# Batch 0 of an adaLN block: modulation of the first batch computed on all partitions, and a new order of its work

## What is computed

```python
mod = (_silu(L0_c) @ L0_wmod).reshape(L0_c.shape[0], 6, 1, -1)
sa, ca, ga, sb, cb, gb = (mod[:, 0], ..., mod[:, 5])
ga = (2 * (ga >= 0) - 1) * jnp.maximum(jnp.abs(ga), 0.25)      # gb likewise
h = _layernorm(x, axis=-1) * (1 + ca) + sa
x = x + ga * attn(h)     # attn: layernorm(gamma, beta), Q K V = h @ W_in + b, rotary on K and V,
                         # A = sum over rows of cos_sim(K) * cos_sim(V), (0.5 * A + 0.5) * Q @ W_out + b, + h
h = _layernorm(x, axis=-1) * (1 + cb) + sb
x = x + gb * ffn(h)      # relu(h W_up) W_down + sum(top-2 softmax weights) * (h W_expert)
```

## Time and profile before

| | us |
|---|---|
| median of 3 runs | 402.54 |
| the runs | 398.53, 402.54, 403.09 |
| the profiled execution | 401.57 |
| its span, first to last instruction | 399.8 |
| PE busy in it | 357.4 |
| DVE, ACT, POOL busy | 250.6, 169.4, 114.2 |
| mean granted clock of TensorE | 0.96 |

### The profile page before, as it was taken

How to read it: one execution, slowest core, us unless ns; L and a number is a source line. 1 busy time by engine, 2 the same in 40 slices (tenths; PEclk the granted TensorE clock), 3 DMA queues, 4 the chain that set the end, 5 groups by cost and what they waited for, 6 DMA issues and landing times.

```text
span 399.8 us, 4571 instructions
## 1 busy us (share of the span) xinstructions
PE 357.4 (89%) x1620; PEld 280.7 (70%) x1620; DVE 250.6 (63%) x512; ACT 169.4 (42%) x307; POOL 114.2 (29%) x114
## 2 busy tenths in 40 slices
PE   4639773099999799998999999999999999999996
PEld 0138462088788588886878887888788878887886
DVE  0784490766998848888597846863852556074454
ACT  1364740858441772117611775227323611361220
POOL 0370920115784252832536222460001000100000
PEclk9959998579999989999999999999999999999999
DMA  7899306503002000000001000300200020011002
GB/s 233 323 356 406 137 13 201 210 2 141 17 2 80 0 0 2 7 22 1 0 2 26 2 0 0 107 26 2 79 26 2 26 79 2 0 52 55 0 2 106
DMA packets 10967, 27.43 MB, mean 69 GB/s; under 512 B 1200, under 2 KB 1584, under 8 KB 9792
## 3 DMA queue, kind: packets, MB, share of 16 engines
q1 hardware_dynamic: 10944, 27.13, 18.9%
HBM read 22.90 MB, written 4.23 MB: 68 GB/s over the span
## 4 chain that ended last, share of the span: by engine, by line
PE 64%; DVE 12%; issue 10%; ACT 6%; POOL 4%; DMA 4%; SPq 1%; DVEq 0%; POOLq 0%; ACTq 0%
PE ps L1081 19%; PE ps L1082 18%; PE ps L1083 18%; PE ps L1120 3%; PE ps L1088 2%; DMA xs<-in_X 2%; POOL w_lo L337 2%; ACT sqj L467 1%; DVE prod L754 1%; DVE hst L702 1%; DMA xs<-in_wmod 1%; ACT ps L528 1%; POOL hrs L334 1%; PE ps L1234 1%; PE ps L1235 1%
## 5 line engine op out<-in xcount | busy, mean ns | idle before, releaser
L1081 PE MATMUL ps<-w_hi,t_hi 128*128 128x512 f32 x192 | 75.9, 396 | 1.1 <-DVE prod L749 1.1
L1082 PE MATMUL ps<-w_lo,t_hi 128*128 128x512 f32 x192 | 75.1, 391 | 0.0
L1083 PE MATMUL ps<-w_hi,t_lo 128*128 128x512 f32 x192 | 75.0, 391 | 0.0
L1081 PE MATMUL ps<-t_hi,w_hi 128*128 128x512 f32 x128 | 52.8, 412 | 15.8 <-DVE sb_col L954 15.8
L1081 PE MATMUL ps<-w_hi,g_hi 128*128 128x512 f32 (+1 forms) x132 | 51.4, 389 | 0.4 <-DVE g_lo L790 0.3
L1082 PE MATMUL ps<-t_lo,w_hi 128*128 128x512 f32 x128 | 51.3, 401 | 0.0
L1083 PE MATMUL ps<-t_hi,w_lo 128*128 128x512 f32 x128 | 51.3, 401 | 0.0
L1083 PE MATMUL ps<-w_hi,g_lo 128*128 128x512 f32 (+1 forms) x132 | 50.6, 383 | 0.0
L1082 PE MATMUL ps<-w_lo,g_hi 128*128 128x512 f32 (+1 forms) x132 | 50.5, 383 | 0.0
L1081 PEld LDWEIGHTS ps<-w_hi,t_hi 128*128 128x128 f32 x192 | 36.3, 189 | 9.4 <-issue 2.0
L730 DVE TENSOR_TENSOR t_lo<-ps,t_hi 128x512 fp32r<-128x512 f32 x28 | 19.2, 690 | 36.0 <-ACT t_hi L530 35.9
(11 more groups left out here) (141 smaller groups left out, 603.5 us busy)
## 6 DMA issues: line engine op xcount, KB each, us to landing
stage<-in_w SPq DMA_DIRECT2D x4, 1024.0 KB, 5.3
out<-xs SPq DMA_DIRECT2D x15, 256.0 KB, 2.0
xs<-in_X SPq DMA_DIRECT2D x3, 1024.0 KB, 8.1
xs<-in_wmod SPq DMA_DIRECT2D x8, 256.0 KB, 6.0
stage<-in_w SPq DMA_DIRECT2D x8, 256.0 KB, 7.7
stage<-in_wmod SPq DMA_DIRECT2D x2, 1024.0 KB, 12.1
gate_bc<-mod_rows SPq DMA_DIRECT2D x8, 256.0 KB, 3.3
xs<-in_X SPq DMA_DIRECT2D x2, 512.0 KB, 6.3
```

Of the source, the lines that this page charges most:

```text
L1081: mm(dst, l_hi, r_hi, start=start, stop=False)
L1082: mm(dst, l_hi, r_lo, start=False, stop=False)
L1083: return mm(dst, l_lo, r_hi, start=False, stop=stop)
```

## The change

Scale and shift of batch 0 are computed on 128 partitions at once: `sc0` holds silu(c) of batch 0, each element repeated over 128 stationary columns, and `mod_first` multiplies it with the modulation weights into banks 2 and 3. ACT adds 1 to the scale in place (`ca1_s`). `mod_pair` makes the rows of all batches for storing, 32 stationary columns for each of two column groups of the array. One ACT pass over 64 partitions copies both, adding 1 to the first 32 through `row_bias`. The copies L917 and L600 and `broadcast0` go.

POOL alternates rstd and low parts from the first tile on and makes the query's low parts (`low_q`) within batch 0's attention. ACT and DVE get a written-out `first_attention`. PE transposes tile 1 inside K/V tile 0 and the chunks of batch 1 earlier. Raw query weights and modulation block 2 swap their places (slots 3 and 2 of xs), the gate rows move to `stage`, the query weights are loaded behind the modulation blocks, X of batch 1 ahead of the biases, X of batch 2 right behind `mod_rest` (`mod_ps` 2), X of batch 3 behind `wlo_q`. `bo_bc` gets a semaphore of its own.

```diff
         acc = sb("acc", [P, D + 2 * ROT])
-        rows = v_sb[0:B]
-        mod_raw, mod_abs, mod_sign, gate_rows = (xs[:, ((B - 1) * NT + i) * D:((B - 1) * NT + i + 1) * D] for i in range(4))
+        sc0 = prod[:, 0:D].rearrange("p (k m) -> p k m", k=NC)
...
+        row_bias = xsum[0:64, 0:1]
...
-
-
-        w_raw = (stage[:, 0, :], stage[:, 1, :], x_slot(2), stage[:, 0, :], stage[:, 1, :], stage[:, 0, :], stage[:, 1, :])
+        MODS = ((2, x_slot(2)), (5, gate_bc[:]), (4, stage[:, 0, :]), (3, stage[:, 1, :]))
+
+
+        w_raw = (stage[:, 0, :], stage[:, 1, :], x_slot(3), stage[:, 0, :], stage[:, 1, :], stage[:, 0, :], stage[:, 1, :])
...
                     sp.dma_start(w_raw[i][:, k * D:(k + 1) * D], w[i][:, k * D:(k + 1) * D]).then_inc(wkv_in[k][i], 16)
-            sp.wait_ge(mod_sb, 2)
-            sp.dma_start(mod_rows[ROW_CA], rows[:, 0, :]).then_inc(row_out, 16)
-            sp.dma_start(mod_rows[ROW_SA], rows[:, 1, :]).then_inc(row_out, 16)
...
 
-            load_x(1)
-            sp.wait_ge(mod_ps, 2)
+            sp.dma_start(MODS[1][1], wmod[MODS[1][0]]).then_inc(wm_in[MODS[1][0]], 16)
+            sp.wait_ge(mod_sb, 1)
+            sp.dma_start(mod_rows[ROW_CA], rows[0:B, :]).then_inc(row_out, 16)
+            sp.dma_start(mod_rows[ROW_SA], rows[32:32 + B, :]).then_inc(row_out, 16)
             sp.dma_start(MODS[0][1], wmod[MODS[0][0]]).then_inc(wm_in[MODS[0][0]], 16)
             sp.wait_ge(row_out, 32)
             load_modulation(1)
-            sp.dma_start(MODS[1][1], wmod[MODS[1][0]]).then_inc(wm_in[MODS[1][0]], 16)
-            sp.dma_start(w_raw[2], w[2]).then_inc(w_in[2], 16)
             sp.wait_ge(wlo_k, NC)
             sp.dma_start(MODS[2][1], wmod[MODS[2][0]]).then_inc(wm_in[MODS[2][0]], 16)
             sp.wait_ge(wlo_v, NC)
             sp.dma_start(MODS[3][1], wmod[MODS[3][0]]).then_inc(wm_in[MODS[3][0]], 16)
-            sp.dma_start(bo_bc[:], brow[0:1, 2 * D:3 * D].to_broadcast([P, D])).then_inc(const_in, 16)
-            sp.wait_ge(mod_ps, 3)
+            sp.dma_start(w_raw[2], w[2]).then_inc(w_in[2], 16)
+            sp.dma_start(bo_bc[:], brow[0:1, 2 * D:3 * D].to_broadcast([P, D])).then_inc(bo_in, 16)
+            sp.wait_ge(mod_ps, 2)
+            load_x(2)
             sp.dma_start(w_raw[3], w[3]).then_inc(w_in[3], 16)
...
                 sp.dma_start(gate_bc[:, b * D:(b + 1) * D],
                              mod_rows[ROW_GA, b:b + 1, :].to_broadcast([P, D])).then_inc(ga_in, 16)
             sp.wait_ge(wlo_q, NC)
-            load_x(2)
+            load_x(3)
             sp.wait_ge(modt_ps, 1)
-            load_x(3)
...
-                    scale_rows(1, 0)
-                    scale_rows(1, 1)
-                    scale_rows(1, 2)
+                    for t in range(NT):
+                        scale_rows(1, t)
+                    rstd_h(1, 0, 2)
+                    low_q(0)
+                    low_q(1)
                     weight(b, 1)
-                    scale_rows(1, 3)
-                    rstd_h(1, 0, 2)
+                    rstd_h(1, 2, 2)
+                    low_q(2)
+                    low_q(3)
                     weight(b, 2)
-                    rstd_h(1, 2, 2)
                     weight(b, 3)
                     rstd_x(2)
                 else:
...
-            pool.wait_ge(cst, 4)
+            pool.wait_ge(cst, 3)
             rstd_x(0)
             low_kv(0, 0)
+            rstd_h(0, 0, 1)
             low_kv(1, 0)
-            rstd_h(0, 0, 1)
+            rstd_h(0, 1, 1)
             low_kv(0, 1)
-            rstd_h(0, 1, 1)
+            rstd_h(0, 2, 1)
             low_kv(1, 1)
-            rstd_h(0, 2, 1)
+            rstd_h(0, 3, 1)
             low_kv(0, 2)
-            rstd_h(0, 3, 1)
             low_kv(1, 2)
-            low_part(2, whi, (1,) * NC, wlo_q)
             for b in range(B):
                 attention(b)
             rstd_h(B + 1, 0, NT)
...
+            def first_attention():
+                norm_sums(0, 0)
+                normalise_x(1)
+                t0_evac(2)
+                t0_evac(3)
+                split_hi(2)
+                norm_sums(0, 1)
+                normalise(1, 0, 2)
+                act.wait_ge(mod_ps, 2)
+                nc.scalar.activation(mod_abs, ps[:, MOD_BANK, :], ACT.Abs, scale=2.0).then_inc(abs_s, 1)
+                act.wait_ge(abs_s, 1)
+                nc.scalar.activation(mod_raw, ps[:, MOD_BANK, :], ACT.Copy).then_inc(mod_row_s, 1)
+                normalise(1, 2, 2)
+                x_sums(2)
+                norm_sums(0, 2)
+                split_hi(3)
+                t_evac(1, 0)
+                norm_sums(0, 3)
+                t_evac(1, 1)
+                x_squares(2)
+                t_evac(1, 2)
+                t_evac(1, 3)
+                normalise_x(2)
+
...
-            act.wait_ge(mod_ps, 2)
-            nc.scalar.activation(rows[:, 1, :], ps[0:B, 1, :], ACT.Copy).then_inc(mod_sb, 1)
-            for k in range(3):
+            act.wait_ge(cst, 5)
+            act.wait_ge(bc_ps, 1)
+            nc.scalar.activation(ps[:, 2, :], ps[:, 2, :], ACT.Identity, bias=half[:, 0:1], scale=half[:, 0:1]).then_inc(ca1_s, 1)
+            for k in range(2):
                 split_hi_kv(0, k)
                 split_hi_kv(1, k)
+            split_hi_kv(0, 2)
             normalise(0, 0, 1)
+            act.wait_ge(mod_ps, 1)
+            nc.scalar.activation(rows, ps[0:64, MOD_BANK, :], ACT.Identity, bias=row_bias, scale=half[0:64, 0:1]).then_inc(mod_sb, 1)
+            split_hi_kv(1, 2)
+            split_hi_kv(0, 3)
             t0_evac(0)
             normalise(0, 1, 1)
-            split_hi_kv(0, 3)
             split_hi_kv(1, 3)
             normalise(0, 2, 1)
             t0_evac(1)
             normalise(0, 3, 1)
-            split_hi(2)
-            t0_evac(2)
-            t0_evac(3)
-            for b in range(B):
+            first_attention()
+            for b in range(1, B):
                 attention(b)
 
             def ffn(b):
                 x2_out(b, 1)
                 o_evac(b, 3)
...
+            def first_attention():
+                x_stats(1)
+                t0_split(1)
+                x_aggr(1)
+                dve.wait_ge(const_in, 32)
+                dve.wait_ge(row_out, 32)
+                x_shift(1)
+                kv_rows(0, 0)
+                kv_products(0, 0)
+                kv_sum(0, 0)
+                h_row(1, 0)
+                h_row(1, 1)
+                h_stats(1, 0)
+                h_stats(1, 1)
+                h_aggr(1, 0, 2)
+                t0_split(2)
+                kv_rows(0, 1)
+                h_row(1, 2)
+                h_row(1, 3)
+                h_shift(1, 0, 2)
+                t0_split(3)
+                h_stats(1, 2)
+                h_stats(1, 3)
+                h_aggr(1, 2, 2)
+                kv_products(0, 1)
+                h_shift(1, 2, 2)
+                kv_sum(0, 1)
+                mod_gates()
+                kv_rows(0, 2)
+                kv_products(0, 2)
+                mod_cols()
+                kv_sum(0, 2)
+                x_mean(2)
+                kv_rows(0, 3)
+                t_split(1, 0)
+                kv_products(0, 3)
+                t_split(1, 1)
+                kv_sum(0, 3)
+                a_pairs(0)
+                x_var(2)
+                t_split(1, 2)
+                t_split(1, 3)
+                x_shift(2)
+                for k in range(NC):
+                    split_lo_out(k)
+
             def attention(b):
...
+            v.memset(xsum[0:32, 0:1], 1.0).then_inc(cst, 1)
+            v.memset(xsum[32:64, 0:1], 0.0).then_inc(cst, 1)
...
+            first = col[:, COL_C:COL_C + NC * B].rearrange("p (k b) -> p k b", k=NC)[:, :, 0:1]
+            v.tensor_tensor(sc0, sc_t[:, 2, :].rearrange("p (k b) -> p k b", k=NC)[:, :, 0:1].to_broadcast([P, NC, P]),
+                            first.to_broadcast([P, NC, P]), ALU.mult).then_inc(c_steps, 1)
...
-            dve.wait_ge(mod_ps, 1)
-            v.tensor_scalar(rows[:, 0, :], ps[0:B, 0, :], 1.0, None, ALU.add).then_inc(mod_sb, 1)
...
-            dve.wait_ge(bc_ps, 1)
+            dve.wait_ge(ca1_s, 1)
...
-                h_stats(0, t)
...
             h_row0(0)
+            h_stats(0, 0)
             h_aggr(0, 0, 1)
-            h_row0(1)
-            h_aggr(0, 1, 1)
-            h_shift(0, 0, 1)
-            h_row0(2)
-            h_aggr(0, 2, 1)
-            h_shift(0, 1, 1)
-            h_row0(3)
-            h_aggr(0, 3, 1)
-            h_shift(0, 2, 1)
+            for t in range(1, NT):
+                h_row0(t)
+                h_shift(0, t - 1, 1)
+                h_stats(0, t)
+                h_aggr(0, t, 1)
             t0_split(0)
             h_shift(0, 3, 1)
             split_lo_kv(0, 3)
             split_lo_kv(1, 3)
-            t0_split(1)
-            for b in range(B):
+            first_attention()
+            dve.wait_ge(ga_in, B * 16)
+            for b in range(1, B):
                 attention(b)
```

(90 more changed lines are left out.)

59 lines of the change are left out of this document (11 added, 48 removed).

## The result

The changed kernel takes 385.54 us in the median of 4 runs (383.56 to 386.50) against 401.36 before in its company: ratio 0.961, 95% interval 0.953 to 0.968. It is faster by 3.9%, inside the range of 376 to 388; the gain is 15.8 us where I had forecast 21.3 (402.54 to 381.2). The profiled execution took 386.50, its span is 384.7.

The account below looks back on a forecast made before the run. Bound taken: PE's hole before batch 0's second Q chunk, then the start's chain; behind the mark, matmuls. Hole 18.2 and start 3.5, less 0.4 of longer waits, gave 21.3 us: 402.54 to 381.2, so 381; range 376 to 388.

Parts of the forecast that it names:

- The hole: PE idle before batch 0's second Q chunk, from the late load of X of batch 2: 15.8 + 2.4 clock = 18.2 us.
- the mark: First K/V matmul of batch 1, the point by which the forecast sums: 92.84 before, forecast 71.5.
- The start: Batch 0 before its first K/V matmul: straight products bring it to 23.2 from 27.91; 3.5 of 4.7 us remain.
- The transfers: Load queue order: query weights behind the modulation blocks, so mod_rest can start near 39.5, with PE waiting 2.3 us.
- both covers: Margins of 1.5 us: row_out lands before VectorE wants it, ca and sa rows before POOL wants them.
- Contention in the middle: Batch 0's attention: four h_row steps slowed 1.1 us each beside POOL, 4.4 us, of which about 1 is slack.
- The block behind the mark: Everything after the first K/V matmul of batch 1 moves whole and keeps its length, 307 us.
- VectorE and ScalarE become the bound: Rival: added waits chain through both engines, slow clock may return; mark 75 to 78, 384.5 to 387.5 us; chance 0.25.
- five signs of being wrong: First K/V matmul after 26, mod_rest after 42, matmuls 0.43 apart after 30, mark after 76, end over 310 behind it.
- The hole only moves: Rival: something else on the path comes as late as 79; 396 to 399 us; chance 0.04.
- slower: Rival: SyncE's queue blocks ahead of three modulation blocks; landing at 75 gives 413 us; chance 0.01.

Follow-up runs that it names:

- e1: Kernel before, with only the load of X of batch 2 moved early, right behind the output weights' load: 387.85 us, ratio 0.971.
- e8: Changed kernel with the load of X of batch 2 put back to its old late place: 397.46 us, ratio 0.994.
- e3: Changed kernel, order untouched, one-column h_shift rewritten as a tensor_scalar with one tensor and a scalar operand: 383.67 us, ratio 0.960.
- e7: e3 with POOL's four low parts of the query weights moved behind both rstd_h of batch 1: 381.75 us, ratio 0.954.
- e9: e6 with POOL's low parts started right behind scale_rows, ScalarE's two weight splits moved, VectorE's tile 1 products one step later: 379.54 us, ratio 0.948.
- e6: e7 with VectorE and ScalarE reordered in batch 0's attention: 382.02 us, ratio 0.954.
- e10: The changed kernel itself timed again, beside e9 on one chip: 386.11 us, ratio 0.964.
- e2: Changed kernel with h_shift of the tile before put back behind h_aggr in batch 0's start: 382.44 us, ratio 0.958.
- e4: Changed kernel with t0_split of tile 2 moved between the two h_row steps of batch 1: 384.48 us, ratio 0.963.

## Why the prediction was right, and which term was mis-sized

**The hole** (18.2 us with its clock): right in cause and place, mis-sized. e1 and e8 show it from both sides as 14.2 and 12.8 us at the mark and 12.2 and 11.4 in the medians. What is missing is a wait of 1.8 that stays (e1) and the 2.4 us of clock, which the kernels pay elsewhere: e1 has eleven slow matmuls at new places, the change ten from 27.29, where I had counted five, and nine from 48.96, where I had counted none.

**The start** (3.5 us of lead at tile 1): this is the step that failed. I put `h_row0` at 14.9 and it started at 16.10, as the shift weights landed later: PE waited 1.95 for them, and the second product ended at 16.00. The scaled rows would not have let it start before 15.83 either. And I priced h_shift as free in its new place. It isn't: three times about 1 us under POOL's low parts. Together 4.1 us at the first K/V matmul (27.29 for 23.2) and 4.6 at tile 1. The prediction had the rule of the Trainium skill (SBUF — State Buffer, "Who interferes with whom") on two SBUF inputs, and applied it to the 512-column steps of the middle alone. e3 shows that this was the whole error between the first row and the first K/V matmul: I had 8.3 us there, the change took 11.19, and e3, which alters h_shift alone, 8.17. The 3.70 of a 128-column product against the 3.60 of the 4-column one shows that this price was right.

**The transfers** (mod_rest near 39.5, both covers 1.5 us): held. The last modulation block landed at 30.91 + 7.3 = 38.2, ahead of PE, which came at 41.97; the row store and the ca and sa rows were in time. With tile 1 later, the wait of 2.3 that I had put there vanished, so PE had 2 of the 4.6 us back at this point. VectorE had not: its kv_rows of tile 0 came at 37.99 instead of 32.9, the split of tile 2 ended at 48.81 instead of 41.8, and PE lost them again in the 3.35 before tile 2.

**Contention in the middle** (4.4 us, of which 1 slack): mis-sized as well. It is 6.6 us of VectorE, as kv_sum and the rotary steps are caught too. I had left kv_sum out, taking one SBUF input as safe in any form. The share that reaches the mark isn't shown by itself: e7 moved the disturbance without moving the mark. With the slow clock of tile 2's first nine matmuls (3.72 us, behind the 3.35 wait, where nine take 2.05 at the fast clock: 1.7 lost), tile 3 comes at 56.46 instead of 51.6, and the mark at 78.35 instead of 71.5.

**The block behind the mark**: right, 306.35 for 307.

**The sum.** The 21.3 to the mark came as 14.5, 6.8 too much. From the first shifted row to the mark I had 56.6 us and it took 62.25. So 1.2 of the 6.8 is the late first row, 2.4 is h_shift (e3: 59.89), and the remaining 3.3 lie in the middle, of which e9 gives back 2.6 with another order.

**The rivals.** The median is outside my own 379.5 to 384 and inside the span of "VectorE and ScalarE become the bound", 384.5 to 387.5, which had 0.25; the mark of 78.35 is 0.35 beyond that rival's 75 to 78. Its mechanism came in part: waits for VectorE before tile 2 and before a transpose (3.35 and 1.80), and the slow clock behind the first. But 2.4 us of the lateness come from h_shift, which that rival doesn't name, so that the number fell into its span is partly luck. Three of my five signs of being wrong came true: the first K/V matmul after 26, matmuls 0.43 us apart after 30, and a mark later than 76. The stated range held because it had the rival in it. "The hole only moves" and "slower" had no part.

## What to carry to other kernels

When an engine waits at one late step, walk the queue of the engine that issues the load before rewriting anything: one moved load gave three quarters (12.2 of 15.8 us) of what a rewritten batch gave. When a small two-input VectorE step is moved, ask what GpSimd is running at its new place: here the price was the rest of that instruction, 1 us for a step of 0.2. Read an edit from an event in front of it and not from the start of the span, as the first loads alone moved everything by up to a microsecond. And of a new order, time the pieces: e6 and e9 have the same idea, and with the four low parts and two splits of ScalarE in other places the mark differs by 3.8 us and the median by 2.5.

## What the runs showed of the hardware

A step of 128 x 1 elements costs 1.21 us with two SBUF tensors beside a GpSimd instruction of 1.26, and 0.22 with one tensor and a scalar operand. A `tensor_scalar` of 768 columns with one SBUF tensor was slow beside GpSimd as well (1.55 against 0.60), and the 128 x 1 one was not; what tells these two apart was not tried. Undisturbed, the 768 columns take 0.60 us with one tensor and 1.02 with two (kv_sum of the later tiles).

TensorE's level followed what it had done before, and not always at once. After the 3.35 us without work before K/V tile 2, matmuls 0.43 us apart (1.2 GHz) came in every kernel that has this wait: right away in the changed kernel (nine from 48.96), in e10 and in e2, but in e3 and e8 only behind three or four at 0.23 (2.4 GHz), from 47.02 and 49.40. After 2.39 us (e7) they came behind two fast ones. After 0.31 (e4), 1.12 (e9), 1.28 (e6) and 1.14 us (the kernel before) at the same place none came. Before the transposes of the modulation rows a wait of 2.17 us in the kernel before was followed by none, and one of 2.20 in e1 by slow transposes and matmuls (53.93 to 57.3). So the wait alone doesn't say whether and when the slow matmuls begin, and what does was not tried.
